# All four expert chunks of a batch in one full-array section, the expert bias beside the second scores, a turned mask in two buffers, and a new order of the first steps

## The chip, the cores and the metric

The kernel runs on one core of one Trainium2 chip. The metric is the device time of one execution in microseconds; of several runs the median is taken.

## The reference

A transformer block with adaptive layer norm over x of 16 batches, 256 tokens, 128 channels, all in fp32:

```
mod = silu(c) @ wmod -> sa, ca, ga, sb, cb, gb per batch (|ga|, |gb| at least 0.25)
h = layernorm(x) * (1 + ca) + sa
q, k, v = h @ Wqkv + bqkv                       # 16 heads of 8
K = exp(-r_sigma * (|k|^2 + |q|^2 - 2 k.q))      # no softmax: a Gaussian kernel
x = x + ga * ((K @ v) @ Wproj + bproj)
h = layernorm(x) * (1 + cb) + sb
gamma = softmax(h @ w_router.T + b_router)       # 8 experts
mask = the two largest of gamma, as 0 or 1
x = x + gb * sum over experts e of mask[e] * (h @ w_experts[e].T + b_experts[e])
```

## The kernel before

The five engines run programs of their own, written out by hand and tied by semaphores. Each program calls `step(k)` for k = -2 to 14, then `last()` for batch 15 and `tail()`. A step is a software pipeline over batches: step k computes the scores and exponentials of batch k, and beside them the projection of batch k-1, second norm and router of batch k-2, the experts of batch k-3, the bias and gate of batch k-4, and ahead of these the first norm and queries and keys of batch k+2 (GpSimd's `first_norm` of k+3). The order of the calls within `step` is the order in which each engine's queue works; nothing overtakes.

TensorE (PE). The four groups of scores of a batch, `qk_scores(k, g)`, each fill all four banks of `scores` with 8 matmuls on 32-row tiles (the trace's `32*128`). ScalarE empties them with two exponentials each, `exp(k, g, 0)` and `exp(k, g, 1)`, and TensorE waits for the first before it starts the next group and for the second before its third matmul. Attention times values (`pv`), queries and keys (`qk_rows`), `norms`, `values`, `router` and `project` work on 128-row, 32-column tiles (`128*32`); the experts and the turns (`turn_x`, `turn_x2`, `turn_mask`) use the array in full height and width. The expert bias is a matmul over 16 rows, `expert_bias`. An expert chunk is one call `experts(b, c)`: three matmuls of 512 columns (the high and low parts of the split weights and activations) into the bank that `f_bank` gives; four chunks make a batch. A PSUM bank is shared by several of these: chunk 1 lies in `att_ps`, where `pv` collects the heads, so chunk 1 stands between `heads_out` and `pv(k, 0)`.

VectorE (DVE) multiplies each chunk with the mask and accumulates it (`experts`, four instructions a chunk), copies the turned mask to SBUF (`mask_rows`), adds the norms' low parts (`norm_rows`), reads out queries and keys (`queries_keys`, `high_parts`), takes the logits and chooses, adds the residual, and normalises for the second norm. ScalarE (ACT) does the exponentials and small copies and norms between them (`norm_high`, `heads_out`, `keep_bias`, `first_norm`, `second_norm`). GpSimd (POOL) squares and splits queries and keys (`parts`), weighs the projection with the gate (`weigh(k)`, which waits for `project(k-1)`), computes the rstd (`rsqrt`), normalises for the first norm (`first_norm`) and applies the gate (`gate`). SyncE (SP) issues the DMAs: x, the stacked rows of queries and keys with their norms (`stack`), the gate rows and the stores.

Of the names that the prediction uses: k is the step, NB is 16, NC (chunks) 4, HE 4, STEPS 16 (VectorE's accumulations a batch, counted by `acc_step`), WIDE 13 (batches below it use the 512-column chunks).

## Time and profile before

| what | value |
|---|---|
| median of three runs | 225.05 us (223.19 to 225.72) |
| the profiled execution's own time | 224.27 us |
| its span in the trace | 222.4 us |
| PE busy | 207.9 us, 93% of the span |
| DVE busy | 173.2 us, 78% |
| ACT busy | 161.8 us, 73% |
| POOL busy | 155.5 us, 70% |
| mean granted clock of TensorE | 0.992 |

The span runs from the first to the last instruction of the profiled execution; the time of an execution has about 1.9 us around it. Busy times are of instructions as the profiler records them. TensorE's matmuls are pipelined, so a matmul's recorded duration overlaps the next one; distances between starts tell what a group costs. PE busy is therefore no measure of how near TensorE is to its peak.

### The profile page before, as it was taken

To read this page: it belongs to the slowest core of one execution; us is meant where nothing else is said; L and a number is where in the kernel's file an instruction comes from. 1 tells how busy PE (TensorE), PEld (TensorE's weight loads), DVE (VectorE), ACT (ScalarE), POOL (GpSimd) and SP (SyncE) were. 2 spreads that over 40 slices of the span, in tenths; PEclk is the share of its full clock that TensorE was granted. 3 is DMA by queue.
4 is the path that set the end of the run, shared out by engine and by line. 5 is a ranking of instruction groups with operands and counts; after the bars stand their busy time and mean duration, and the time that the engine had idled before them with its cause. 6 is when DMAs were issued, how large, how long until landed. Compare 5 with 4: busy or idle time off the path is not lost.

```text
span 222.4 us, 7993 instructions
## 1 busy us (share of the span) xinstructions
PE 207.9 (93%) x3084; PEld 138.7 (62%) x3084; DVE 173.2 (78%) x595; ACT 161.8 (73%) x233; POOL 155.5 (70%) x230
## 2 busy tenths in 40 slices
PE   7976869899999999999999999999999999989993
PEld 7553425466666676666666666666766767555792
DVE  4776703267989898898979898989898988897884
ACT  5228775888877878879796969697888788656362
POOL 4456955656596969696979889797979663745183
PEclk9999997999999999999999999999999999999999
DMA  4564233433332434342415151424223243000001
GB/s 147 154 208 153 97 124 95 142 115 109 99 116 68 144 98 144 93 149 73 163 52 192 30 182 41 155 84 137 102 84 131 71 143 99 3 24 27 3 24 47
DMA packets 22470, 22.91 MB, mean 103 GB/s; under 512 B 2330, under 2 KB 20258, under 8 KB 22434
## 3 DMA queue, kind: packets, MB, share of 16 engines
q1 hardware_dynamic: 21962, 21.79, 30.3%
q10 hardware_dynamic: 472, 0.62, 0.8%
q8 instruction: 25, 0.41, 0.8%
q14 instruction: 11, 0.09, 0.1%
HBM read 6.65 MB, written 2.12 MB: 39 GB/s over the span
## 4 chain that ended last, share of the span: by engine, by line
PE 82%; DVE 6%; POOL 4%; issue 3%; ACT 2%; DMA 1%; POOLq 0%; ACTq 0%
PE att_ps L1073 23%; PE scores L1053 11%; PE qkv_ps L1092 8%; PE ffn_ps L1250 4%; PE mid_ps L1148 3%; PE qkv_ps L1250 3%; PE ffn_ps L1252 3%; PE ffn_ps L1251 3%; PE mid_ps L1103 3%; PE qkv_ps L1116 3%; ACT probs L539 2%; PE scores L1005 2%; PE qkv_ps L1252 2%; PE qkv_ps L1251 2%; PE mid_ps L1162 1%
## 5 line engine op out<-in xcount | busy, mean ns | idle before, releaser
L539 ACT ACTIVATE probs<-scores 128x1024 f32<-128x1024 f32 x128 | 124.3, 1022 | 32.1 <-PE scores L1053 30.8
L1073 PE MATMUL att_ps<-probs,vpad 128*32 128x256 f32 x1024 | 65.5, 383 | 0.1
L1073 PEld LDWEIGHTS att_ps<-probs,vpad 128*32 128x32 f32 x1024 | 33.1, 111 | 16.8 <-issue 1.3
L1053 PE MATMUL scores<-st 32*128 32x256 f32 x512 | 35.3, 332 | 5.2 <-ACT probs L539 3.8
L435 POOL TENSOR_TENSOR sq<-qkf 128x512 f32<-128x512 f32 x15 | 15.6, 1040 | 31.9 <-DVE qkf L793 31.9
L1053 PEld LDWEIGHTS scores<-st 32*128 32x128 f32 x512 | 20.8, 183 | 21.1 <-issue 11.9
L768 DVE SCALAR_TENSOR_TENSOR acc<-ffn_ps,mask,acc 128x128 f32<-128x128 f32 x102 | 28.4, 340 | 0.0
L399 POOL TENSOR_SCALAR xn<-x_all,stats,rstd 128x128 f32<-128x128 f32 x30 | 24.3, 815 | 1.6
L394 POOL TENSOR_TENSOR rstd<-ve,expo 128x2 f32<-128x2 f32 x32 | 22.9, 715 | 2.5
L793 DVE TENSOR_TENSOR qkf<-qkv_ps,bqk_col 128x512 f32<-128x512 f32 x16 | 11.1, 692 | 12.0 <-PE qkv_ps L1092 10.8
L437 POOL TENSOR_TENSOR hl<-qkf,hl 128x512 fp32r<-128x512 f32 x15 | 19.2, 1282 | 0.0
L1092 PE MATMUL qkv_ps<-h,wqk_sb 128*32 128x256 f32 x256 | 18.8, 416 | 0.0
L765 DVE TENSOR_SCALAR acc<-qkv_ps,mask 128x128 f32<-128x128 f32 x26 | 7.9, 346 | 11.7 <-PE qkv_ps L1252 11.7
L748 DVE BATCH_NORM_STATS2 stats<-x_all 128x6 f32<-128x256 f32 x32 | 13.7, 427 | 0.6
L1250 PE MATMUL ffn_ps<-we_hi,h_hi 128*128 128x512 f32 (+1 forms) x30 | 14.0, 465 | 0.0
L427 POOL TENSOR_TENSOR x_all<-x_all,rb_all 128x256 f32<-128x256 f32 x16 | 12.8, 799 | 0.0
L392 POOL TENSOR_TENSOR ve<-stats,eps 128x2 f32<-128x2 f32 x32 | 6.3, 197 | 8.9 <-DVE stats L748 8.9
L425 POOL TENSOR_TENSOR wg<-wproj_sb,rb_all 128x128 f32<-128x128 f32 x16 | 7.8, 487 | 6.0 <-PE mid_ps L1148 5.9
L408 POOL TENSOR_TENSOR gated<-acc 128x256 f32<-128x256 f32 x13 | 9.7, 748 | 2.6 <-DVE acc L768 2.6
L1252 PE MATMUL ffn_ps<-we_lo,h_hi 128*128 128x512 f32 (+1 forms) x30 | 11.4, 379 | 0.0
L1251 PE MATMUL ffn_ps<-we_hi,h_lo 128*128 128x512 f32 (+1 forms) x30 | 11.4, 379 | 0.0
L411 POOL TENSOR_TENSOR gated<-gated,bias_sb 128x256 f32<-128x256 f32 x13 | 9.6, 736 | 2.5 <-ACT bias_sb L569 1.6
(188 smaller groups left out, 416.3 us busy)
## 6 DMA issues: line engine op xcount, KB each, us to landing
st<-hl SPq DMA_DIRECT2D x47, 256.0 KB
rb_all<-rb_rows SPq DMA_DIRECT2D x16, 192.0 KB, 3.4
out_dram<-x_all SPq DMA_DIRECT2D x16, 128.0 KB, 3.1
x_all<-in_L_attn_x_dram SPq DMA_DIRECT2D x13, 128.0 KB, 3.2
st<-norm_parts SPq DMA_DIRECT2D x60, 16.0 KB
we_sb<-in_L_ffn_w_experts_dram SPq DMA_DIRECT2D x1, 512.0 KB, 6.0
w_mod_sb<-in_L_wmod_dram SPq DMA_DIRECT2D x1, 256.0 KB, 5.3
st<-hl ACTq DMA_DIRECT2D x1, 256.0 KB
```

The source lines that it names most:

```text
L394: nc.gpsimd.tensor_tensor(rstd[:, n, :], ve[:, n, :], expo[:, :], ALU.pow).then_inc(rstd_ok, 1)
L399: i = nc.gpsimd.tensor_scalar(xn[:, par, t * C:(t + 1) * C], x_all[:, b, t * C:(t + 1) * C], stats[:, 0, par, 3 * t + 1:3 * t + 2], rstd[: ...
L435: nc.gpsimd.tensor_tensor(sq[:, :, :], qkf[:, :, :], qkf[:, :, :], ALU.mult).then_inc(sq_ok, 1)
L437: nc.gpsimd.tensor_tensor(hl[:, 1:4:2, :], qkf[:, :, :], hl_f[:, 0:4:2, :], ALU.subtract).then_inc(lo_ok, 1)
L539: nc.scalar.activation(probs[:, g, 2 * half:2 * half + 2, :], scores[:, 2 * half:2 * half + 2, :], ACT.Exp, scale=two_sigma).then_inc((exp ...
L768: v.scalar_tensor_tensor(a, y, m, a, ALU.mult, ALU.add).then_inc(acc_step, 1)
L1053: i = pe.matmul(scores[:, r, t * T:(t + 1) * T], st[rows, par, g, t * P:(t + 1) * P], st[rows, par, g, T:2 * T], start=True, stop=True)
L1073: i = pe.matmul(att_ps[r * ROWS:(r + 1) * ROWS, 0:T], heads[:, g * ROWS:(g + 1) * ROWS], probs[:, g, r, t * T:(t + 1) * T], start=(g == 0 ...
L1092: i = pe.matmul(qkv_ps[m, a * T:(a + 1) * T], wqk_sb[:, a, m], h1[:, b % 2, :], start=True, stop=True)
L1250: pe.matmul(dst, hi, we_hi[:, es], start=True, stop=False)
L1251: pe.matmul(dst, lo, we_hi[:, es], start=False, stop=False)
L1252: i = pe.matmul(dst, hi, we_lo[:, es], start=False, stop=True)
```

## The change

It moves work within the engines' lists and alters waits with it; no arithmetic changes.

- In a step from k = 3 on, TensorE works through all four chunks of batch k-3 in one section with the two turns of x, behind the second scores. Before, chunks 0 to 2 stood there and chunk 3 at the end of the step. The banks of the chunks are dealt anew (`f_bank`), and `pv(k, 0)` and `qk_rows` wait for one chunk more.
- `turn_mask` moves up behind the first scores, `expert_bias` behind the second scores; the turned mask `mask_t` gets two buffers. VectorE's `mask_rows` goes ahead of `norm_rows`, and its fourth chunk is taken right behind the third.
- From step 3 on, the projection goes from between the fourth scores and the product to the end of the list, `values` behind the second product, and the router stands ahead of them.
- ScalarE copies the bias between the two exponentials of group 1.
- In the first steps: the x of batches 4 and 5 are both loaded at k = 0; GpSimd normalises batches 2 and 3 before it weighs; the first norms of steps 1 and 2 go ahead of `parts`; `qk_rows(2)` stands behind the first scores of step 1 instead of ahead of them, with one product between the first and second and one behind the second scores; VectorE splits the expert weights and bias in step 1 instead of steps -1 and 0.

```diff
@@ PSUM banks and buffers
-        mask_t = sb("mask_t", [2 * NE, T], F32R)
+        mask_t = sb("mask_t", [2 * NE, 2, T], F32R)
...
-                return ((qkv_ps, att_ps, ffn_ps, ffn_ps) if b < NB - 4 else (qkv_ps, ffn_ps, qkv_ps, ffn_ps))[c][:, :]
+                return ((ffn_ps, qkv_ps, att_ps, ffn_ps) if b < NB - 4 else (qkv_ps, ffn_ps, qkv_ps, ffn_ps))[c][:, :]
@@ SyncE
-                if k >= 0 and has(k + 4):
-                    sp.dma_start(x_all[:, k + 4, :], xv[k + 4]).then_inc(ld_xb[k % 2], 16)
+                for b in (4, 5) if k == 0 else (k + 4,):
+                    if k >= 0 and k != 1 and has(b):
+                        sp.dma_start(x_all[:, b, :], xv[b]).then_inc(ld_xb[b % 2], 16)
@@ GpSimd (EARLY = 2)
                     parts(1)
                     first_norm(2)
-                    weigh(0)
                     first_norm(3)
                 if has(k - 4):
                     gate(k - 4)
+                if 0 < k <= EARLY:
+                    first_norm(k + 3)
                 if has(k + 2):
                     parts(k + 2)
-                if k > 0:
+                if has(k):
                     weigh(k)
...
-                if k > 0 and has(k + 3):
+                if k > EARLY and has(k + 3):
                     first_norm(k + 3)
@@ ScalarE
-                if k > 0:
+                if k > 1:
                     norm_high(k + 1)
-                if has(k - 1):
+                if k > 1:
                     heads_out(k - 1)
+                exp(k, 1, 0)
                 if has(k - 4):
                     keep_bias(k - 4)
-                exp(k, 1, 0)
                 exp(k, 1, 1)
-                if k == 0:
+                if k == 1:
+                    heads_out(k - 1)
+                if k <= 1:
                     norm_high(k + 1)
...
-                if k == 0:
-                    first_norm(k + 2)
...
                 exp(k, 3, 1)
+                if k == 0:
+                    first_norm(k + 2)
@@ VectorE (the expert bias' parts move from expert_weights to split_weights)
                 if k == 0:
                     first_stats(2)
+                if k == 1:
+                    first_stats(4)
+                if has(k - 3):
+                    mask_rows(k - 3)
                 if has(k + 1):
                     norm_rows(k + 1)
                 if has(k - 3):
-                    mask_rows(k - 3)
-                    experts(k - 3, 0)
-                    experts(k - 3, 1)
-                    experts(k - 3, 2)
+                    for c in range(NC):
+                        experts(k - 3, c)
                 if k == 0:
                     values(1)
                     first_stats(3)
+                if k == 1:
                     split_weights()
...
-                if k > 0 and has(k + 3):
+                if k == 1:
+                    first_stats(5)
+                if k > EARLY and has(k + 3):
                     first_stats(k + 3)
...
-                if has(k - 3):
-                    experts(k - 3, 3)
@@ TensorE, waits
                             if 3 <= b < NB - 1:
-                                pe.wait_ge(acc_step, STEPS * (b - 3) + 2 * HE)
+                                pe.wait_ge(acc_step, STEPS * (b - 3) + 3 * HE)
...
                 if b >= 5:
-                    pe.wait_ge(acc_step, STEPS * (b - 5) + HE)
+                    pe.wait_ge(acc_step, STEPS * (b - 5) + 2 * HE)
...
-                if b >= 3:
-                    pe.wait_ge(h2_ok, b - 2)
+                if b >= 4:
+                    pe.wait_ge(logit_ok, b - 2)
+                elif b == 3:
+                    pe.wait_ge(h2_ok, 1)
...
                 if b < NB - 4 and c == 0:
+                    pe.wait_ge(m_sb, b + 1)
+                elif b < NB - 4 and c == 1:
                     pe.wait_ge(norm_ok, b + 5)
-                elif b < NB - 4 and c == 1:
+                elif b < NB - 4 and c == 2:
                     pe.wait_ge(o_ok, b + 3)
-                elif b < NB - 4 and c == 2:
-                    pe.wait_ge(m_sb, b + 1)
                 elif b < NB - 4:
-                    pe.wait_ge(acc_step, steps(b, 3 * HE))
+                    pe.wait_ge(acc_step, steps(b, HE))
@@ TensorE, the order of a step
                 qk_scores(k, 0)
-                if has(k - 4):
-                    expert_bias(k - 4)
-                if k == 0:
+                if has(k - 3):
+                    turn_mask(k - 3)
+                if k <= 1:
                     qk_rows(k + 1)
                 if k > 1:
                     norms(k + 1)
                 if has(k - 1):
                     pv(k - 1, 2)
+                if k > 1:
                     pv(k - 1, 3)
+                qk_scores(k, 1)
+                if has(k - 4):
+                    expert_bias(k - 4)
                 if k == 1:
-                    norms(k + 1)
-                if has(k - 3):
-                    turn_mask(k - 3)
-                qk_scores(k, 1)
-                if k == 0:
+                    pv(k - 1, 3)
+                if k <= 1:
                     norms(k + 1)
                 if has(k - 3):
                     experts(k - 3, 0)
...
                 if has(k - 3):
                     experts(k - 3, 2)
+                    experts(k - 3, 3)
                 qk_scores(k, 2)
...
                 pv(k, 0)
-                values(k + 1)
+                if k < 3:
+                    values(k + 1)
                 if k == 0:
                     turn_x(k + 2)
                 if has(k - 2):
                     router(k - 2)
                 qk_scores(k, 3)
+                if k >= 3:
+                    pv(k, 1)
+                    values(k + 1)
                 if has(k - 1):
                     project(k - 1)
-                pv(k, 1)
+                if k < 3:
+                    pv(k, 1)
                 if k == NB - 2:
                     turn_mask(k - 2)
-                if k == 0:
-                    qk_rows(k + 2)
-                if has(k - 3):
-                    experts(k - 3, 3)
```

## Rows read from the trace of the kernel before

**Rows 1.** Busy by stage (steps 7, 14): us, PE, PEld, DVE, ACT, POOL, clock, DMA.

```profile
96.85:108.62 11.77, 11.76 (x189) 7.85 (x188) 10.29 (x37) 9.57 (x13) 9.66 (x16) 1.00 0.36 114
179.17:190.40 11.23, 11.11 (x175) 7.63 (x174) 9.17 (x36) 9.26 (x13) 5.37 (x11) 1.00 0.28 96
```

**Rows 2.** TensorE's timeline in step 7: start, length, instructions, idle time before in brackets.

```profile
96.85 0.51 PE L1053 MATMUL scores<-st 32*128 32x256 f32 x8
...
97.45 0.43 PE L1116 MATMUL qkv_ps<-sq,nw 128*32 128x128 f32 x8
...
99.76 0.51 PE L1053 MATMUL scores<-st 32*128 32x256 f32 x8
100.19 0.51 PE L1250 MATMUL qkv_ps<-we_hi,h_hi 128*128 128x512 f32 x1
...
100.99 0.40 PE L1250 MATMUL att_ps<-we_hi,h_hi 128*128 128x512 f32 x1
...
101.70 0.38 PE L1162 MATMUL mid_ps<-ident,x2n 128*128 128x128 f32 x2
...
102.93 0.51 PE L1053 MATMUL scores<-st 32*128 32x256 f32 x8
...
105.12 0.62 PE L1103 MATMUL mid_ps<-wqkv_sb,h 128*32 128x128 f32 x16
105.56 0.29 PE L1172 MATMUL mid_ps<-wr_t,h 128*32 128x8 f32 x16
105.77 0.51 PE L1053 MATMUL scores<-st 32*128 32x256 f32 x8
106.29 0.64 PE L1148 MATMUL mid_ps<-wg,o_sb 128*32 128x128 f32 x16
106.72 1.07 PE L1073 MATMUL att_ps<-probs,vpad 128*32 128x256 f32 x16
107.72 0.50 PE L1250 MATMUL ffn_ps<-we_hi,h_hi 128*128 128x512 f32 x1
...
108.62 0.51 PE L1053 MATMUL scores<-st 32*128 32x256 f32 x8
```

**Rows 3.** ScalarE's timeline: pairs of exponentials in steps 0, 1, 2 and 7.

```profile
18.55 1.94 ACT L539 ACTIVATE probs<-scores 128x1024 f32<-128x1024 f32 x2 [0.49 <-PE scores L1053]
...
26.84 1.94 ACT L539 ACTIVATE probs<-scores 128x1024 f32<-128x1024 f32 x2 [0.49 <-PE scores L1053]
...
39.90 1.94 ACT L539 ACTIVATE probs<-scores 128x1024 f32<-128x1024 f32 x2 [0.50 <-PE scores L1053]
...
103.47 1.94 ACT L539 ACTIVATE probs<-scores 128x1024 f32<-128x1024 f32 x2
```

**Rows 4.** TensorE's timeline in steps 0 and 1.

```profile
18.11 0.50 PE L1053 MATMUL scores<-st 32*128 32x256 f32 x6 [0.53 <-ACT probs L539]
...
20.54 0.50 PE L1053 MATMUL scores<-st 32*128 32x256 f32 x6 [0.53 <-ACT probs L539]
...
23.48 0.44 PE L1135 MATMUL mid_ps<-ident,xn 128*128 128x128 f32 x2 [1.00 <-POOL xn L399]
...
33.07 1.94 PE L1092 MATMUL qkv_ps<-h,wqk_sb 128*32 128x256 f32 x16
```

**Rows 5.** Busy time by stage, as rows 1, around the slower clock.

```profile
32.80:36.30 3.50, 3.50 (x38) 1.65 (x38) 1.04 (x2) 2.10 (x3) 0.46 (x1) 0.51 0.38 122
```

**Rows 6.** VectorE's timeline: values in step 0; residual, chunk 3 and mask copy in step 7.

```profile
22.54 0.42 DVE L817 TENSOR_TENSOR vpad<-mid_ps,bq_all 128x256 f32<-128x256 f32 x1 [1.44 <-PE mid_ps L1103]
...
95.74 0.41 DVE L825 TENSOR_TENSOR x_all<-mid_ps,x_all 128x256 f32<-128x256 f32 x1
...
97.21 1.10 DVE L768 SCALAR_TENSOR_TENSOR acc<-ffn_ps,mask,acc 128x128 f32<-128x128 f32 x4
...
99.86 0.41 DVE L841 CAST mask_t<-ffn_ps 16x256 fp32r<-16x256 f32 x1
```

**Rows 7.** The page's slices: TensorE's granted clock in tenths, 40 slices of the span.

```profile
PEclk9999997999999999999999999999999999999999
```

16 lines of the change are left out of this document (8 added, 8 removed).

## The prediction

> **What bounds the kernel now.** I read the profile by stages, since the kernel is a start, a pipeline of 16 equal batches and an end. The busy times of one step of the pipeline come first: in the step from 96.85 to 108.62 us TensorE is busy 11.76 of 11.77 us, VectorE 10.29, ScalarE 9.57, GpSimd 9.66 [rows 1]. TensorE sets that step. The timeline of TensorE in the same step shows it working through its list with no idle bracket at all [rows 2]. I divide the step at its four groups of scores, because each of them hands ScalarE two exponentials (together 1.94 us, [rows 3]) and the next group of scores may overwrite its banks only after they are done. The four distances are 2.91 us (96.85 to 99.76), 3.17 (to 102.93), 2.84 (to 105.77) and 2.85 (to 108.62) [rows 2]. The question for the change is not only how much TensorE work it removes, but in which of these four distances.
>
> How short can a distance get? In the first step ScalarE sets the pace: the six matmuls that need the second exponential start at 18.11 and again at 20.54 after 0.53 us idle, which is a cycle of 2.43 us: 0.44 from these matmuls to the first exponential (18.55), 1.94 of exponentials, 0.05 back [rows 3, 4]. When the eight matmuls of a group run without a stop, the first exponential starts 0.54 after them (102.93 to 103.47), so the distance behind an undisturbed group is at least 0.54 + 1.94 + 0.05 = 2.53 us [rows 2, 3]. All four distances now are above that.
>
> The early steps are another matter. The exponentials of batch 1 begin at 26.84 and those of batch 2 at 39.90, so this step takes 13.06 us [rows 3]. In it the granted clock is 0.51 from 32.8 to 36.3, about the lower of its two levels (1.2 against 2.4 GHz), and the 16 matmuls of the queries and keys, started at 33.07, take 1.94 us [rows 4, 5]. In step 0 the turn of x, at 23.48, waits 1.00 us for GpSimd's normalised rows [rows 4].
>
> **The change part by part: the steady step** (k from 4 to 13, ten steps). TensorE's new list, priced by distances of starts in rows 2.
>
> First distance: scores, turned mask, norms, two attention products. The bias product leaves. Before, scores and bias took 0.60 (96.85 to 97.45); now the scores stand alone at 0.43 (as 99.76 to 100.19). Norms, products and mask keep 2.31 (97.45 to 99.76). Sum 2.74, 0.17 less.
>
> Second distance: scores and bias 0.60, first chunk 0.80 (100.19 to 100.99), then everything up to 102.93 as before (1.94), then the fourth chunk. A chunk inside a full-array section is 0.71 (100.99 to 101.70). Sum 0.60 + 0.80 + 1.94 + 0.70 = 4.04, which is 0.87 more.
>
> Third distance: the values (0.44, 105.12 to 105.56) go. TensorE alone would need 2.40. ScalarE's bound is 2.53, and that is what counts: 0.31 less.
>
> Fourth distance: before, scores 0.52 (with some 0.08 of waiting for the logits), projection 0.43, product 1.00 and the lone chunk 0.90 (107.72 to 108.62). Now scores 0.43, product 0.86, values 0.44, projection about 0.55 with its way out, in all 2.29. The lone chunk cost 0.90 against 0.70 in company. ScalarE's cycle after scores that had to wait is 2.43: 0.42 less.
>
> Sum over TensorE's work alone: 2.74 + 4.04 + 2.40 + 2.29 = 11.47, which is 0.30 under 11.77. Sum with ScalarE: 2.74 + 4.04 + 2.53 + 2.43 = 11.74, only 0.03 under. So the saved changes of tile shape are real, but the fourth chunk is taken from a distance that then falls under ScalarE's bound and is put into one that has ScalarE idle anyway. Ten steps give 0.3 us. The prices of the mask behind scores and of the bias ahead of a chunk are not shown by rows in this order; I take their neighbours' and allow 0.06 a step each way, 0.6 us in all.
>
> A rule that speaks to these changes. The same three matmuls take 0.90 where they stand alone and 0.71 inside a section, and the product ahead of the lone chunk needs 1.00 where the work itself is some 0.86 (102.93 to 105.12 is scores, 0.44, and two groups of 16 such matmuls, 1.75: queries and keys 0.89, product 0.86), so entering and leaving the full array costs about 0.1 each time [rows 2]. The Trainium skill, TensorEngine Tiling (Array Packing), section Tiling Modes, says that changing the tiling mode, and not just the tile, drains TensorE; by that rule alone the ten steps would give 3 us. The trace agrees that there is a price; what it is worth is another question, and the rule's own result is the second rival below.
>
> Waits inside the steady step. VectorE takes the chunks in turn, four accumulations in 1.10 us each, of which the next hides 0.07 [rows 6]. Its first begins about 1.0 us after the start of chunk 0, so chunk 0 is read out before chunk 3 wants its bank (0.5 us to spare), chunk 1 before the queries and keys of the next batch (0.7), chunk 2 before the next product (0.6). VectorE has no work more than before. The projection moves to the end of the list, just ahead of the next scores, and behind it hang the residual, the second norm's statistics, GpSimd's weighting and rstd, the normalised rows and only then the turned mask's copy, which chunk 0 now waits for. Before, residual to mask copy was 4.12 us (95.74 to 99.86), with the fourth chunk (1.03) and the norm rows (0.26) in between, which both go [rows 6]: 2.8 us remain, 0.4 more for the copy. The residual starts some 0.16 after the next scores do, so the copy is there at 3.3, and chunk 0 is due at 2.74 + 0.60 = 3.34. It just fits. I price this at nothing, with the third rival in mind. ScalarE's moves (bias copy between the exponentials of group 1) lie in its idle time of the long second distance.
>
> **Steps 3 and 14, and the end.** Step 3 has no bias yet: nothing. Step 14 (11.23 us, rows 1) has no queries and keys and its bias product sits in the third distance. There the fourth chunk lengthens the second distance by 0.87 as well; first distance 2.74, second 3.82, third 2.53 (ScalarE again), fourth 2.51 with the last turned mask: 11.60, so 0.37 more. The end is not edited, but its first turn of x2 needs rows that hang on the late projection of step 14; between nothing and one chunk (0.9, rows 2) I take 0.3 more.
>
> **The early steps.** Step 0: the statistics of batch 2 no longer stand behind VectorE's work on the expert bias, and GpSimd normalises it before the weighting. GpSimd is free 0.5 us sooner; then the turn of x waits for VectorE to have read the values (its add ends at 22.96, [rows 6]) instead of for GpSimd: from 23.48 to 23.02, 0.46 less. The second x load moves one step up on SP's queue, ahead of the stacking of batch 1; an issue is about 0.45 us and the low parts behind it come later anyway, so nothing. ScalarE's h of batch 2, moved behind the last exponential, fits into the 0.44 between scores and exponential.
>
> Step 1, by the four distances. First: scores, queries and keys, one product is 2.19 + 0.11 for leaving (102.93 to 105.12 is the same work), under ScalarE's 2.43. Second: product 1.00, norms 0.24, turn of x 0.36 and scores 0.43, again under 2.43; the squares that the norms need come from GpSimd 0.3 earlier than wanted, where the old order kept TensorE idle. Third: TensorE waits until ScalarE has copied heads and norms and made h of batch 3 (0.93 after the scores), then queries and keys 0.89, product 0.86 and values with their way out 0.55: 3.24. Fourth: 2.53. Sum 10.63 against 13.06, so 2.43 less. About 1.5 of it is the half-speed stretch: at full speed those 1.94 us would be 1.07 and the product behind would lose as much. I take it that it goes, because the 3 us ahead of the drop hold a product and most of a group of queries and keys more in the new order. VectorE's 3.4 us of splitting the expert weights move into step 1, ahead of its work on batch 3's queries and keys. By this count that work starts between 34 and 34.9, and the norms that need it come at 37.0; the split hides, with 0.2 us to spare.
>
> Step 2 keeps its four distances.
>
> **Sum.** 224.27 (the profiled execution; its span is 222.4 and 1.9 lies around it) - 0.46 - 2.43 - 0.3 + 0.37 + 0.3 = 221.75. The median of the three runs is 225.05, 0.78 above the profiled execution, and the three spread over 2.5 us, so I place the forecast a little above the sum: 222.0.
>
> **The rivals.**
> First, the half-speed stretch stays or comes at another place. For it: the new order of step 0 still leaves TensorE idle up to 0.9 us before the second exponential. Against: the stretches with that much idle before 26 us kept full clock, and the page shows only this drop [rows 7]. Price 1.5 us: 223.5. Chance 0.16. The Trainium skill, TensorE: Matmul & The Clock Gate, Part 1, says that the throttled state is the default and activity releases it; the trace shows the drop after the stretch with the least TensorE work.
> Second, ScalarE doesn't bind and the drains saved count in full: 0.27 more in each of ten steps, 219.0. For it: ScalarE is idle 0.9 us before most exponentials. Against: rows 4 show the cycle of 2.43 when nothing else holds. Chance 0.11.
> Third, the other side: the late projection. If the way from projection over rstd to the mask copy is longer than my 3.3 us, chunk 0 waits, and the second distance, which has no slack, grows by all of it. It decides from 0.05 us on. At 0.3 us a step it costs 3 us and eats the gain: 224.8; at 0.6, with the drop of the clock kept, 229. For it: the fit is within 0.1 us, and the same instructions of VectorE and GpSimd vary with what the other does. Chance 0.17, of which 0.08 ends above 227.3.
> Fourth, the early reorder brings only the 0.46 of step 0, because another wait (the stacked rows' DMA or the split weights) holds step 1: 224.2. Chance 0.12.
> The forecast itself, 221.0 to 223.2, has 0.44.
>
> **How the numbers follow.** The range must take in 8 of 10: from 219.2 (most of the second rival) to 225.2 (the first, the fourth and the middle of the third). Differences under about 1% can't be told from no change here; 1% faster is 222.8. Faster: 0.9 of the forecast's 0.44, the second rival and a fifth of the first, 0.54. Slower than 227.3: 0.08 to 0.09. The rest, 0.37, is no change.
>
> **What would show it.** In the new trace the step of 11.77 should be 11.7 to 11.8; scores at distances of about 2.7, 4.0, 2.5 and 2.4; TensorE with idle brackets of 0.1 to 0.2 us on ScalarE's exponentials before the fourth and the first scores of a step, where it has none now. The exponentials of batches 1 and 2 should be 10.6 apart, without a stretch at half clock. Step 14 should be near 11.6. If chunk 0 shows an idle bracket that names the mask copy, the third rival is at work; a step of 11.5 would be the second. The forecast is wrong as a whole if the early gain doesn't come, since nearly all of it lies there.

## The result, and the profile after

| | before | after |
|---|---|---|
| median of the runs taken together | 224.12 us (4 runs, 223.09 to 225.72) | 226.56 us (4 runs, 225.15 to 227.78) |
| the profiled execution | 224.27 us, span 222.4 | 225.99 us, span 224.1 |
| its mean granted clock | 0.992 | 0.985 |

The ratio is 1.0107, 95% interval 1.0054 to 1.016: the change makes the kernel about 1% slower. The forecast was 222.0 us, 1.4% faster, and the range ended at 225.2. Here and below, ratios and their intervals leave out executions more than 1.5% above the fastest of their kernel (two of six of the early order alone, three of six of the same with the norm rows first, one each of four others: the mask copy first, that early order filled, the turn of the mask moved, and the kernel before beside the first experiments), while medians take in all.

The span is best compared by steps. A step is taken here from the third matmul of its first scores (the one that waits for ScalarE's second exponential) to that of the next. The last 0.05 us, closing semaphores, are left out.

| stretch | before | after | forecast for after |
|---|---|---|---|
| start to the first scores | 15.58 | 14.64 | as before |
| step 0 | 10.82 | 12.22 | 10.36 |
| step 1 | 13.06 | 10.69 | 10.63 |
| step 2 | 10.45 | 11.80 | as before |
| step 3 | 11.60 | 11.56 | as before |
| steps 4 to 13, each | 11.77 | 11.81 | 11.74 |
| step 14 | 11.23 | 12.23 | 11.60 |
| from the first scores of batch 15 to the end | 31.90 | 32.79 | 32.2 |

The differences are -0.94, +1.40, -2.37, +1.35, -0.04, +0.40 (ten steps), +1.00 and +0.89, in all 1.69 us; the spans differ by 1.7. The code of the first 14 us is the same in both, so the 0.94 of the start belongs to no edit. Nearly all of it lies in one group, the first queries and keys, which start at 7.23 us in both and take 1.90 us before and 1.07 after (TensorE's timeline).

```profile
7.23 1.90 PE L1092 MATMUL qkv_ps<-h,wqk_sb 128*32 128x256 f32 x16
```

```profile
7.23 1.07 PE L1099 MATMUL qkv_ps<-h,wqk_sb 128*32 128x256 f32 x16
```

Over all kernels below, the start varied from 14.2 to 15.6 us and this group from 1.07 to 1.94: up to 14.7 us where it took 1.07 us, from 15.4 where it took 1.87 or more. What makes it long is open: the same 16 matmuls take 1.94 us at half clock in step 1 [rows 4, 5], but here the granted clock is recorded as 1.00.

The steady step first: busy times of the new steps 7 and 14, as [rows 1]. These two stretches begin at the first matmul of a group that stops in its middle, so they are longer than the steps by their third matmuls (step 14 by 0.12 us).

```profile
96.20:108.02 11.82, 11.79 (x194) 8.12 (x190) 10.44 (x36) 9.60 (x14) 9.77 (x14) 1.00 0.33 114
178.90:191.25 12.35, 11.34 (x180) 7.92 (x176) 8.66 (x34) 9.47 (x14) 5.17 (x8) 1.00 0.28 97
```

And TensorE's timeline in step 7, as [rows 2].

```profile
96.20 0.63 PE L1060 MATMUL scores<-st 32*128 32x256 f32 x8
...
99.06 0.51 PE L1060 MATMUL scores<-st 32*128 32x256 f32 x8
99.40 0.33 PE L1217 MATMUL mid_ps<-be_parts,mask_t 16*128 16x128 f32 x2
99.76 0.47 PE L1259 MATMUL ffn_ps<-we_hi,h_hi 128*128 128x512 f32 x1
...
103.17 0.51 PE L1060 MATMUL scores<-st 32*128 32x256 f32 x8
...
105.57 0.64 PE L1060 MATMUL scores<-st 32*128 32x256 f32 x8
...
108.02 0.39 PE L1060 MATMUL scores<-st 32*128 32x256 f32 x2
```

By the third matmul of each group the distances are 2.74, 4.11, 2.53 and 2.43 us (by first matmuls they look like 2.86, 4.11, 2.40, 2.45, since a group that is stopped in its middle starts early). The third and the fourth are ScalarE's cycle to the hundredth: its pairs of exponentials begin at 103.72, 106.15 and 108.58, 2.43 apart, idle 0.49 between them. The records show the stop not as a bracket but as the first row of a group that is 0.63 us long instead of 0.51.

From the bias product (99.40) to chunk 0 (99.76) there are 0.36 us; in a run below, where nothing holds the chunk, there are 0.26. VectorE's timeline of these moments shows what it waits for.

```profile
98.12 0.42 DVE L855 TENSOR_TENSOR h_lo<-h,h_hi 128x256 fp32r<-128x256 f32 x1
98.69 0.60 DVE L837 TENSOR_SCALAR x2n<-x_all,stats,rstd 128x128 f32<-128x128 f32 x2
99.21 0.41 DVE L843 CAST mask_t<-ffn_ps 16x256 fp32r<-16x256 f32 x1
```

The mask copy ends at 99.62 and stands behind the normalising, which can't start before GpSimd's rstd ends at 98.66. In step 14 the same wait is in the open, and behind it a product waits for VectorE's accumulations (TensorE's timeline; before, the step had neither bracket). The second wait costs nothing: the third distance of the step, where it lies, is 2.53 us before and after.

```profile
182.99 0.47 PE L1259 MATMUL ffn_ps<-we_hi,h_hi 128*128 128x512 f32 x1 [0.56 <-DVE mask_t L843]
...
187.31 1.07 PE L1080 MATMUL att_ps<-probs,vpad 128*32 128x256 f32 x16 [0.45 <-DVE acc L770]
```

The early steps: ScalarE's pairs of exponentials in steps 0, 1 and 2, as [rows 3]. The wait of 2.69 us lies in step 0.

```profile
17.61 1.94 ACT L542 ACTIVATE probs<-scores 128x1024 f32<-128x1024 f32 x2 [0.50 <-PE scores L1060]
...
24.86 1.94 ACT L542 ACTIVATE probs<-scores 128x1024 f32<-128x1024 f32 x2 [2.69 <-PE scores L1060]
27.30 1.94 ACT L542 ACTIVATE probs<-scores 128x1024 f32<-128x1024 f32 x2
...
37.99 1.94 ACT L542 ACTIVATE probs<-scores 128x1024 f32<-128x1024 f32 x2 [0.49 <-PE scores L1060]
```

From 27.30 to 37.99 step 1 takes 10.69 us, as forecast, and without a stretch at half clock. But the page's slices, and the busy times of the stretch in question, show that half clock now lies in step 0, and for twice as long.

```profile
PEclk9995899999999999999999999999999999999999
```

```profile
17.40:24.20 6.80, 5.52 (x56) 2.73 (x52) 2.15 (x6) 4.04 (x5) 4.49 (x7) 0.50 0.57 193
```

Step 2 has a new wait. TensorE's timeline first, then VectorE's.

```profile
45.66 0.51 PE L1060 MATMUL scores<-st 32*128 32x256 f32 x8
47.90 0.64 PE L1157 MATMUL mid_ps<-wg,o_sb 128*32 128x128 f32 x16 [1.73 <-DVE logit L862]
```

```profile
41.29 0.60 DVE L837 TENSOR_SCALAR x2n<-x_all,stats,rstd 128x128 f32<-128x128 f32 x2 [2.47 <-POOL rstd L396]
41.80 0.34 DVE L812 SCALAR_TENSOR_TENSOR norm_parts<-norm_hi,lo_col,qkv_ps 128x128 fp32r<-128x128 f32 x1
44.40 0.69 DVE L795 TENSOR_TENSOR qkf<-qkv_ps,bqk_col 128x512 f32<-128x512 f32 x1 [2.25 <-PE qkv_ps L1099]
46.98 0.69 DVE L801 TENSOR_TENSOR hl<-qkv_ps,bqk_col 128x512 fp32r<-128x512 f32 x1 [1.90 <-DMA st<-norm_parts]
47.59 0.17 DVE L862 TENSOR_TENSOR logit<-mid_ps,br_all 128x16 f32<-128x16 f32 x1
```

Read from below: the projection waits for the logits, whose bank it writes; the logits stand on VectorE behind the high parts of batch 4; these wait for the DMAs that stack the norm rows of batch 3, four issues that SP's queue took from 42.17 to 44.93; and these rows (41.80) stand behind the normalising of batch 0, which sat 2.47 us for rstd.

The end: TensorE's first turn of x2 there, and what it waits for on VectorE.

```profile
195.25 0.44 PE L1171 MATMUL mid_ps<-ident,x2n 128*128 128x128 f32 x2 [0.74 <-DVE x2n L837]
```

```profile
191.16 0.42 DVE L827 TENSOR_TENSOR x_all<-mid_ps,x_all 128x256 f32<-128x256 f32 x1 [1.51 <-PE mid_ps L1157]
...
193.64 1.55 DVE L837 TENSOR_SCALAR x2n<-x_all,stats,rstd 128x128 f32<-128x128 f32 x2 [0.27 <-POOL rstd L396]
```

### The profile page after: what moved, and what is told of

Same layout as the page of the kernel before. It is cut to its first block, busy times and chain, and to the rows that moved or that the text cites. A ratio compares the mean times of both kernels' runs of the same rounds, so it can differ in the third digit from the quotient of the medians.

```text
span 224.1 us, 7993 instructions
## 1 busy us (share of the span) xinstructions
PE 207.6 (93%) x3084; PEld 142.1 (63%) x3084; DVE 173.8 (78%) x595; ACT 162.2 (72%) x233; POOL 156.9 (70%) x230
## 4 chain that ended last, share of the span: by engine, by line
PE 75%; POOL 8%; DVE 7%; issue 3%; DMA 3%; ACT 2%; SPq 1%; POOLq 0%; DVEq 0%
PE att_ps L1080 21%; PE scores L1060 11%; PE qkv_ps L1099 6%; PE ffn_ps L1259 4%; PE mid_ps L1112 3%; PE ffn_ps L1261 3%; PE ffn_ps L1260 3%; PE mid_ps L1157 3%; DMA st<-norm_parts 3%; ACT probs L542 2%; DVE acc L770 2%; PE qkv_ps L1125 2%; PE scores L1012 2%; POOL rstd L396 2%; PE mid_ps L1171 2%
## 5 line engine op out<-in xcount | busy, mean ns | idle before, releaser
L1080 PEld LDWEIGHTS att_ps<-probs,vpad 128*32 128x32 f32 x1024 | 31.3, 110 | 19.1 <-issue 1.4
L1060 PE MATMUL scores<-st 32*128 32x256 f32 x512 | 38.2, 335 | 3.1 <-ACT probs L542 1.8
L1060 PEld LDWEIGHTS scores<-st 32*128 32x128 f32 x512 | 23.6, 184 | 21.1 <-issue 15.2
L437 POOL TENSOR_TENSOR sq<-qkf 128x512 f32<-128x512 f32 x15 | 15.6, 1042 | 25.8 <-DVE qkf L795 25.8
L396 POOL TENSOR_TENSOR rstd<-ve,expo 128x2 f32<-128x2 f32 x32 | 25.1, 785 | 2.5
L770 DVE SCALAR_TENSOR_TENSOR acc<-ffn_ps,mask,acc 128x128 f32<-128x128 f32 x78 | 22.4, 342 | 0.0
L767 DVE TENSOR_SCALAR acc<-ffn_ps,mask 128x128 f32<-128x128 f32 x26 | 7.9, 346 | 10.8 <-PE ffn_ps L1261 10.8
L837 DVE TENSOR_SCALAR x2n<-x_all,stats,rstd 128x128 f32<-128x128 f32 x32 | 11.4, 399 | 5.0 <-POOL rstd L396 3.6
L770 DVE SCALAR_TENSOR_TENSOR acc<-att_ps,mask,acc 128x128 f32<-128x128 f32 x48 | 13.4, 342 | 0.0
L875 DVE TENSOR_SCALAR mask<-taken 128x32 fp32r<-128x32 f32 x16 | 12.7, 794 | 0.6
L801 DVE TENSOR_TENSOR hl<-qkv_ps,bqk_col 128x512 fp32r<-128x512 f32 x15 | 10.2, 683 | 3.3 <-DMA st<-norm_parts 3.3
```

The costliest lines, as they stand in the source:

```text
L396: nc.gpsimd.tensor_tensor(rstd[:, n, :], ve[:, n, :], expo[:, :], ALU.pow).then_inc(rstd_ok, 1)
L437: nc.gpsimd.tensor_tensor(sq[:, :, :], qkf[:, :, :], qkf[:, :, :], ALU.mult).then_inc(sq_ok, 1)
L770: v.scalar_tensor_tensor(a, y, m, a, ALU.mult, ALU.add).then_inc(acc_step, 1)
L875: v.tensor_scalar(mask[:, b % 2, :, :, :], taken[:, :, :].unsqueeze(2).broadcast_to([P, NT, 2, NE]), CHOSEN, None, ALU.is_ge).then_inc(mas ...
L1060: i = pe.matmul(scores[:, r, t * T:(t + 1) * T], st[rows, par, g, t * P:(t + 1) * P], st[rows, par, g, T:2 * T], start=True, stop=True)
L1080: i = pe.matmul(att_ps[r * ROWS:(r + 1) * ROWS, 0:T], heads[:, g * ROWS:(g + 1) * ROWS], probs[:, g, r, t * T:(t + 1) * T], start=(g == 0 ...
```

## The experiments

My theory after the result: the loss is four separate things, each with a cause of its own: the norm rows of batch 3 late in step 2, the mask copy behind the normalising (a little in each step, 0.6 us in step 14), the late projection of step 14, which the end waits for, and half clock in step 0, which I put down to TensorE's idle time there. The rival theory: the new order of the steady steps as such is dearer for TensorE than I count (the saved changes of tile shape aren't worth what I took), and what shows as waits would only move elsewhere if mended.

**First, the two halves of the change, and the first two repairs** (timed together; before had a median of 224.97 us beside them).

The early order alone is the kernel before with the edits that mention `EARLY`, k <= 1, k == 0 and k == 1 in the diff; the steady order alone is the changed kernel with these undone.

> The kernel before with only the first steps reordered (loads of x, GpSimd, ScalarE, VectorE and TensorE in steps 0 and 1); the steady step is that of before, 11.77 us. My theory now: of the loss, step 2 is an early one (scores of batch 2 to scores of batch 3 took 11.80 us after against 10.45 before, because the chain from the norms of batch 2 over the stacked rows' DMA to the logits of batch 0 did not come earlier), and step 1 keeps its gain (10.69 against 13.06). Steps 0 to 3 together end within 1 us of before at the same number of slow clock windows: 223 to 224.5 in all. Rival, that the early order is where the whole loss lies: 226 or more. Rival, my prediction's: about 221.5.

> The changed kernel with the order of the first steps put back to that of before. The steady step was 11.81 us after against 11.77 before, step 14 12.23 against 11.23, and the end 32.85 against 32.0: sum +2.3, so this should be about 2.3 us slower than before (226.4), with the same step of 11.81 and distances of scores 2.74, 4.11, 2.53, 2.43. Rival, that the late reorder costs nothing and the loss is the clock's in the first steps: equal to before within 0.5 us.

The mask copy first:

```diff
-                if has(k - 3):
-                    mask_rows(k - 3)
                 if has(k + 1):
                     norm_rows(k + 1)
...
                 if has(k - 2):
                     split_h2(k - 2)
+                    mask_rows(k - 2)
                 if has(k - 1):
                     normalise(k - 1)
```

> The changed kernel with VectorE's copy of the turned mask ahead of the second norm's normalised rows instead of behind them. My theory: chunk 0 waits for this copy, 0.08 us in each steady step and 0.56 us in step 14, because it stands behind GpSimd's rstd. Expected: the second distance 4.03 instead of 4.11 and the step 11.73; step 14 at 11.7 instead of 12.23; 1.3 us less than the changed kernel. Rival, that chunk 0 is late because the bias product ahead of it on the array needs that long to leave: nothing changes in the steady step.

The norm rows first:

```diff
-                if has(k + 1):
+                if has(k + 1) and k != 2:
                     norm_rows(k + 1)
...
+                if k == 1:
+                    norm_rows(3)
                 if has(k - 1):
                     normalise(k - 1)
```

> The changed kernel with VectorE's norm rows of batch 3 ahead of the normalised rows of batch 0 (the first of which waited for nothing but the latter's rstd). My theory: in step 2 the norm rows came at 41.8 us behind that wait, their DMAs landed at 46.9, and behind this landing VectorE's high parts of batch 4 and the logits of batch 0 held the projection 1.73 us. With the norm rows at 40.2 the projection waits 0.2 to 0.5 and the scores of batch 3 come 1.1 us earlier. Rival, that GpSimd's chain holds the step whatever VectorE's order: no change of that distance (3.67 us).

Measured (the steps and the end are those of each kernel's one profiled execution):

| kernel | median us | ratio to before, interval | step 0 | 1 | 2 | 4 to 13 | 14 | end |
|---|---|---|---|---|---|---|---|---|
| early order alone | 223.7 | 0.994 (0.9883 to 0.9996) | 10.41 | 10.69 | 12.32 | 11.76 | 11.23 | 31.92 |
| steady order alone | 226.71 | 1.0098 (1.005 to 1.0146) | 10.82 | 13.04 | 10.44 | 11.81 | 12.23 | 33.90 |
| mask copy first | 223.67 | 0.9981 (0.9922 to 1.0041) | 10.41 | 10.69 | 12.09 | 11.74 | 11.62 | 32.76 |
| norm rows first | 225.0 | 1.0038 (0.9982 to 1.0094) | 11.80 | 10.69 | 10.63 | 11.81 | 12.23 | 32.75 |

The early order gains 0.6%, the steady order loses 1%. Where no half clock falls on it, the early order brings 10.41 and 10.69 us for steps 0 and 1, 2.8 us less than before (whose step 1 holds a half-clock stretch), and gives back 1.6 in step 2 (12.09 in the third row; the 12.32 of the first has 3.41 us of half clock in it, behind which the wait of the projection is hidden). With the norm rows first, step 2 is 10.63 and the wait of the projection is gone, where I had expected 0.2 to 0.5 us of it to stay. With the mask copy first, chunk 0 follows the bias product after 0.26 us (TensorE's timeline, step 7), the ten steps are 0.07 us shorter each and step 14 is 0.61 shorter: 11.62 where I had worked out 11.60.

```profile
98.07 0.51 PE L1059 MATMUL scores<-st 32*128 32x256 f32 x8
98.41 0.33 PE L1216 MATMUL mid_ps<-be_parts,mask_t 16*128 16x128 f32 x2
98.67 0.50 PE L1258 MATMUL ffn_ps<-we_hi,h_hi 128*128 128x512 f32 x1
...
102.11 0.51 PE L1059 MATMUL scores<-st 32*128 32x256 f32 x8
```

The median fell by more than these 1.3 us, from 226.56 to 223.67. The clock goes with that: the profiled execution had no half clock in its early steps, and four of the six had a mean clock of 0.992 or more, against one of four of the changed kernel. The end of 33.90 in the steady order alone holds a stretch of 3.41 us at half clock, from 202.6 on.

**Second, what the steady step is bound by.** In both kernels the exponentials of groups 2 and 3 run over half their columns. The other half is left out, so these kernels compute something else, and each ran once; only the steps are compared.

```diff
-                nc.scalar.activation(probs[:, g, 2 * half:2 * half + 2, :], scores[:, 2 * half:2 * half + 2, :], ACT.Exp,
+                w = NT * T // 2 if g >= 2 and k > 0 else NT * T
+                nc.scalar.activation(probs[:, g, 2 * half:2 * half + 2, 0:w], scores[:, 2 * half:2 * half + 2, 0:w], ACT.Exp,
```

> The changed kernel, in which from batch 1 on the exponentials of the third and fourth group of scores run over 512 of their 1024 columns (the other half of these exponentials is left out). If ScalarE's cycle of 2.43 to 2.53 us is what keeps the third and fourth distance long, both fall to TensorE's own work there: 2.41 and 2.29 us, and the steady step goes from 11.81 to 11.5 to 11.6 us. If instead the saved changes of tile shape never were worth anything in these two distances, or something else holds them (logits, heads, a DMA), the step stays at 11.8 us. The early steps and the end gain as well, so the time as a whole (some 4 to 6 us less) decides nothing; the step does.

> The kernel before with the same half of the exponentials left out. If its steady step is set by TensorE in all four distances, the step stays at 11.75 to 11.78 us although ScalarE has 1.9 us a step less to do; then the two kernels with half exponentials differ by about 0.2 to 0.27 us a step in favour of the changed order, ten steps by 2 to 2.7 us. If ScalarE takes part in the limit of the old order as well, its step falls too, by 0.1 us or more, and the difference is smaller.

The old order keeps 11.76 us: TensorE alone sets it (the first two distances, whose exponentials were left whole, are 2.90 and 3.17, above ScalarE's 2.53). The new order falls from 11.81 to 11.69: that is neither the 11.5 to 11.6 of the expectation nor the 11.8 of its rival. TensorE's timeline shows why:

```profile
96.82 0.51 PE L1061 MATMUL scores<-st 32*128 32x256 f32 x8
...
99.56 0.51 PE L1061 MATMUL scores<-st 32*128 32x256 f32 x8
99.90 0.33 PE L1218 MATMUL mid_ps<-be_parts,mask_t 16*128 16x128 f32 x2
100.39 0.47 PE L1260 MATMUL ffn_ps<-we_hi,h_hi 128*128 128x512 f32 x1 [0.16 <-DVE mask_t L844]
...
103.80 0.51 PE L1061 MATMUL scores<-st 32*128 32x256 f32 x8
...
106.20 0.51 PE L1061 MATMUL scores<-st 32*128 32x256 f32 x8
...
108.52 0.51 PE L1061 MATMUL scores<-st 32*128 32x256 f32 x8
```

The third and fourth distance fell to 2.40 and 2.31, as expected of TensorE's own work. But the first scores no longer stop in their middle, so what follows comes 0.12 us earlier after their start, while the mask copy ends 3.42 us after that start as before. Chunk 0 waits 0.13 us longer: half of the gain went into the mask copy. So the same cut was made once more with the mask copy first.

> The changed kernel with the mask copy ahead of the normalising and, as before, the exponentials of the third and fourth group over half of their columns from batch 1 on (half of these exponentials is left out). In the run with half exponentials alone the third and fourth distance fell to 2.40 and 2.32 us, but the second grew from 4.11 to 4.24, with chunk 0 waiting for the mask copy. If these are the only two things between the step and TensorE's own work, the step is 2.74 + 4.04 + 2.40 + 2.32 = 11.50 us. If something else comes late as soon as the mask copy is there, it stays at 11.6 us or more.

11.61 us, again not all. The distances are 2.74, 4.16, 2.41 and 2.31. Three are TensorE's own; in the second the turn of x stands 0.29 us behind the turn of x2 instead of 0.22, and its neighbour another 0.05, and GpSimd's timeline has the rows for which it waits end at 99.74, just ahead of it.

```profile
99.50 0.38 PE L1171 MATMUL mid_ps<-ident,x2n 128*128 128x128 f32 x2
99.79 0.44 PE L1144 MATMUL mid_ps<-ident,xn 128*128 128x128 f32 x2
```

```profile
98.16 1.58 POOL L401 TENSOR_SCALAR xn<-x_all,stats,rstd 128x128 f32<-128x128 f32 x2
```

So behind ScalarE and the mask copy stands a third cover (something that takes up a gain of TensorE's), GpSimd's way from the projection over the residual's weighting and the two rstd to the normalised rows. It is read from the trace, here and once more below; no run removes it. Without all three, TensorE's list would take 2.74 + 4.04 + 2.41 + 2.31 = 11.50 us, 0.26 less than the old order (this sum is of distances from two runs, not itself run).

**Third, the end.**

```diff
                 qk_scores(k, 3)
+                if k == NB - 2:
+                    project(k - 1)
                 if k >= 3:
                     pv(k, 1)
+                if 3 <= k < NB - 2:
                     values(k + 1)
-                if has(k - 1):
+                if has(k - 1) and k < NB - 2:
                     project(k - 1)
```

(and `values(15)` behind the first product of step 14, where it was before the change.)

> The changed kernel with one step put back: in step 14 the projection of batch 13 stands ahead of the product again, and the values of batch 15 where they stood. If the 0.85 us that the end has grown hang on the late projection of step 14 (residual, statistics, rstd and normalised rows of batch 13 follow it, and the end's first turn of x2 waits for them), the end falls from 32.8 to between 31.9 and 32.2 us, and the wait of that turn for the normalised rows goes. The rival: the end has grown since GpSimd's gate now runs beside VectorE's normalising there, or since the chunks are dealt to other banks; then it stays within 0.2 us of 32.8. Step 14 itself: 12.2 to 12.3 us either way, as its chunk waits for the mask copy.

The end took 31.89 us, as before the change, and the turn of x2 has no bracket left. Step 14 grew to 12.36, a little above the 12.2 to 12.3 expected. VectorE's normalising was 1.56 us long here too, beside GpSimd's gate, and it cost nothing, for it now started a projection's lead earlier: the rival is out. The time of this one run, 228.04 us, is of half clock for 13.7 us in the first 53; its stages afterwards are as the table has them.

**Fourth, the repairs together, and TensorE's idle time filled.** The fill is 3 warm-up matmuls of 128 columns ahead of the first scores, and in a free bank 1, 1 and 2 in step 0 and 4 in step 2.

```diff
+            def fill(n):
+                pe.wait_ge(wet0_sb, 1)
+                warm_up(n, bank=ffn_ps)
...
+                if k == 0:
+                    fill(1)
                 qk_scores(k, 1)
...
                     norms(k + 1)
+                if k == 0:
+                    fill(1)
+                if k == 2:
+                    fill(4)
...
                 if k == 0:
+                    fill(2)
                     turn_x(k + 2)
```

> The changed kernel with both repairs of VectorE's list: the mask copy ahead of the normalising, the norm rows of batch 3 ahead of the first normalising. If the two losses are what they seem, they add: steps of 11.73 us, step 14 at 11.6, step 2 at 10.6 instead of 11.8, so 1.3 us less than the first repair alone where the clock does the same: 222.2 us at a mean clock of 0.992, a median between 221.5 and 223.0 with one half-clock stretch in some runs. The rival: with the wait in step 2 gone a half-clock stretch comes in its place (as in the run with the norm rows first, 225.0), and the median is 223.5 or more.

> The kernel before with the new order of the first steps and the norm rows of batch 3 ahead of the first normalising; the steady steps are the old ones. Against the early order alone (223.7 us, its step 2 12.32 us with a half-clock stretch in it) the wait for the logits goes; step 2 should be 10.6 us without a half-clock stretch and 11.9 with one. Time 221.5 to 223, so 0.99 of before. If the wait was hidden behind the half-clock stretch, nothing is gained on the early order alone.

> As both copies first, and TensorE's idle time in the start and in steps 0 and 2 is filled with warm-up matmuls into a free bank (3 before the first scores, 1 before the second and 1 before the third scores, 2 before the turn of x in step 0, 4 before the turn of x2 in step 2). If the half-clock stretches of the first 50 us come from TensorE's idle time, they go: mean clock of the runs 0.99 to 1.0, and the time is that of both copies first at its best clock, 221.5 to 222.3 us, with less spread. If the stretches don't depend on this idle time, clock and spread stay and the time is the same or up to 0.5 us longer, for the added matmuls.

> As both filled, and the projection of step 14 ahead of the product again. If the end's growth is its doing, 0.5 to 0.9 us less than both filled: 220.7 to 221.7 us; else the same as both filled.

> The changed kernel with nothing but the warm-up matmuls in TensorE's idle time of the start and of steps 0 and 2. If the half-clock stretches of the first 50 us come from that idle time, the mean clock goes from 0.985 to 0.992 or more and the time from 226.6 to 224.5 to 225.3 us; the waits in step 2, for the mask copies and at the end stay. If they don't, it stays at 226 to 227 us.

> The kernel before with the new order of the first steps, the norm rows of batch 3 first, and TensorE's idle time in the start and in steps 0 and 2 filled with the same warm-up matmuls. Its steady steps, its step 14 and its end are those of before: 10 x 11.76 + 11.22 + 31.9. Against both filled with the early projection of step 14 (221.7 us; 10 x 11.74 + 11.75 + 31.9) that is 0.3 us less: 221.4 us at a mean clock of 1.0. So if the steady change has nothing to give on this chip as it stands, this kernel is as fast or faster, 221.0 to 221.8; if it has, this one is 222 or more. If the half-clock stretches don't come from the idle time, the runs spread from 221 to 225 as with the early order and the norm rows alone.

| kernel | median us (lowest to highest, runs) | ratio to before, interval | mean clocks |
|---|---|---|---|
| both copies first | 223.68 (222.13 to 225.16, 12) | 0.9974 (0.9934 to 1.0014) | 0.977 to 1.0, two of 12 at 1.0 |
| early order, norm rows first | 224.03 (220.91 to 225.27, 6) | 0.9897 (0.9822 to 0.9972) | 0.974 to 1.0 |
| both copies first, filled | 222.68 (221.97 to 224.81, 12) | 0.9951 (0.991 to 0.9992) | 0.981 to 1.0, three at 1.0 |
| the same, early projection in step 14 | 221.7 (221.44 to 222.04, 6) | 0.988 (0.9829 to 0.9931) | 1.0 in five of 6 |
| changed kernel, filled | 225.11 (223.97 to 226.97, 12) | 1.0032 (0.9995 to 1.007) | 0.989 to 1.0 |
| early order, norm rows first, filled | 221.27 (220.64 to 224.94, 6) | 0.9867 (0.9815 to 0.9919) | 1.0 in four of 6 |

Not all expectations came. Both copies first was to be at 221.5 to 223.0 us; at 223.68, with a half-clock stretch in step 2 of its profile, it met its rival's case. The early order with the norm rows first was expected at 221.5 to 223 and both filled at 221.5 to 222.3; their medians lie above. The other three came as expected. The ratio of the second row rests on three executions.

The fill: the changed kernel's median is 225.11 us with it and was 226.56, in four runs on another occasion, without; the intervals of the two ratios overlap, and so they do in the other two pairs of this table with and without the fill. Full clock for the whole span came in no run of four without the fill and three of 12 with it (changed kernel), two of 12 and three of 12 (both copies first), one of six and four of six (early order, norm rows first). So the fill seems to help, and that isn't shown for any one kernel. It doesn't keep half clock away: the profiled executions of the changed kernel filled and of both filled still have one stretch of 3.41 us in step 0 (11.90 and 11.96 us). Step 2 of the changed kernel filled took 12.18 us, not 11.80; why is open. Both copies first, by the stages of its profile: 10.41, 10.69, 12.33 (half clock in it), 11.74 each, 11.62, 32.78; step 2 without half clock is 10.62 in the filled one. With the early projection step 14 is 11.75 and the end 31.90. By stages, then, the repairs add up as worked out; the medians have the clock's draws in them as well.

The last row is the answer on the steady change: with the same repairs of the first steps, the old steady order (11.76 a step, 11.23 in step 14, 31.91 at the end) is 221.27 us and the new one, with its own two repairs, 221.7. The ratios' intervals overlap, so neither is shown to be faster than the other; no gain of the steady change is shown.

**Fifth, work moved under the bound.** On the fully repaired kernel the turn of the mask goes one step earlier, behind the projection.

```diff
-                if has(k - 3):
-                    turn_mask(k - 3)
...
-                if k == NB - 2:
+                if has(k - 2):
                     turn_mask(k - 2)
```

> Both filled with the early projection of step 14 (221.7 us), and the turn of the mask one step earlier, behind the projection: its 0.22 us go from the first distance (2.74 us, above ScalarE's bound) into the fourth (2.43 us, where ScalarE sets the pace and TensorE's own work is 2.3). If the bounds of the distances are as the runs so far show, the step goes from 11.74 to 2.53 + 4.04 + 2.53 + 2.51 = 11.61 to 11.65 us, and the time to 220.4 to 221.0 us. If the turn there waits for the choice of the experts, or ScalarE's bound isn't what holds the fourth distance, the step stays at 11.74 us or grows.

221.92 us (220.55 to 225.2, 12 runs), ratio 0.9889 (0.9851 to 0.9928); steps of 11.74 and 11.83 us by turns. The expected 0.1 us a step didn't come. The distances of step 7 are 2.53, 4.24, 2.53 and 2.53, three of them as expected; the second grew by 0.2: the turn of x, due 0.22 us after the turn of x2, came after 0.38, when GpSimd's normalised rows were there.

```profile
98.60 0.38 PE L1173 MATMUL mid_ps<-ident,x2n 128*128 128x128 f32 x2
98.98 0.44 PE L1146 MATMUL mid_ps<-ident,xn 128*128 128x128 f32 x2
```

```profile
97.34 1.58 POOL L402 TENSOR_SCALAR xn<-x_all,stats,rstd 128x128 f32<-128x128 f32 x2
```

ScalarE's bounds held: the fourth distance took the turn for 0.1 us, the first gave 0.21. The third cover, found with the half exponentials, is what the gain ran into by the trace.

## Why the prediction was wrong, point by point

- **"Step 2 keeps its four distances"** failed: +1.35 us, the largest single error. I followed what step 1 would gain and not what its gain would ask of the next step. TensorE came to step 2 1.9 us sooner; GpSimd, with the first norm of batch 4 now ahead of `parts(3)`, gave rstd 3.7 us after the step's third matmul (41.25 against 37.55) where before it was 0.8 after it. VectorE's norm rows stood behind that, then SP's four issues, the high parts, the logits, the projection. With the norm rows ahead, step 2 was 10.63: the wait is shown to be the cause. That the order of `first_norm(4)` and `parts(3)` is what made rstd late is read from the trace, and wasn't tried alone.
- **"I price this at nothing" (the fit of the mask copy)** failed: the third rival, in a small form, 0.07 us a step, and 0.6 of step 14, which I had left out of that rival. The terms were right and the addition was not: 0.16 to the residual, 2.83 (4.12 - 1.03 - 0.26) and 0.41 for the copy make 3.40, not 3.3, so by its own terms the copy came after the 3.34 at which chunk 0 was due. Measured in step 7: 0.14, 2.87 and 0.41, in all 3.42. The copy ahead of the normalising gave back both, and then the step (11.74) and step 14 (11.62) were the forecast's 11.74 and 11.60.
- **"between nothing and one chunk (0.9, rows 2) I take 0.3 more" (the end)** was mis-sized: 0.89. It was the upper bound that held, and the cause was the one named, the late projection of step 14.
- **Half clock: "I take it that it goes"** held for step 1 and failed for the kernel. In the profiled execution 6.83 us of half clock lie in step 0, the first rival's case. They cost 1.8 us (12.22 against 10.41 in profiles of the same order without half clock) instead of 1.5. The price of one stretch was right: 3.41 us of half clock made step 0 11.80 to 11.96 instead of 10.41, and step 2 12.33 instead of 10.62, which is 1.4 to 1.7 us.
- **What the half clock belongs to.** How much of it there is differs between executions of one kernel. Of 58 runs of the kernel before, timed beside the experiments, 19 had a mean clock of 0.992 and a median of 223.17 us, 33 had 0.977 and 225.07: a mean clock lower by 0.015 went with 1.9 us more. One stretch of 3.41 us makes 0.992 of this span, as in the profile. But none of the 58 had a higher clock than 0.992, and the three profiles with the old order of the first steps (before, steady order alone, half exponentials) all have a stretch in step 1, beginning between 31.9 and 32.9 us. With the new order of the first steps and no fill, three of 41 runs had full clock (half exponentials not counted). So one stretch seems to belong to the old order, and the new one can lose it; the mistake was to take its loss as sure in every execution and to price nothing for others. That TensorE's idle time brings it isn't shown. The Trainium skill, TensorE: Matmul & The Clock Gate, Part 1, has activity release the throttled state; by that rule the fill should help, and the runs lean that way without showing it.
- **The steady step** was right in its mechanism and, with the mask copy mended, in its size. Distances of 2.74, 4.04, 2.53 and 2.43 were measured for 2.74, 4.04, 2.53 and 2.43. The gain of 0.26 us in TensorE's own work, worked out above as 11.50 against 11.76, is hidden by ScalarE in two distances. The second rival is out as a result, though its price, 0.27 a step, was right. The Trainium skill, TensorEngine Tiling (Array Packing), section Tiling Modes, says that a change of the mode drains TensorE; the traces agree in that the order with one full-array section fewer a step needs these 0.26 us less of TensorE.
- **Steps 0 and 1** were right where the clock was full: 10.41 for 10.36, 10.69 for 10.63, and in step 1 in each distance (2.43, 2.43, 3.30 and 2.53 for 2.43, 2.43, 3.24 and 2.53). But of the 2.4 us of step 1, some 1.5 were the clock's; no profile has the old step 1 at full clock, so this is an estimate from the prices of a stretch above.
- **The sum.** Forecast -2.5 us against the profiled execution, measured +1.7 in it: +1.35 (step 2), +1.86 (step 0), +0.7 (steady steps), +0.63 (step 14), +0.6 (end), less 0.94 of a shorter start, make 4.2.
- **The chances.** The clock (first rival), the mask copy (third) and the end's upper bound were taken as alternatives, one at a time, and a wait for the stacked rows' DMA only for step 1 (fourth). They lie in different steps and nothing ties them; three came true together, and the DMA's wait one step later. Independent risks of one sign belong in the range as a sum.

## What to carry to other kernels

When an edit makes an engine arrive earlier somewhere, the next step must be priced with the other engines where they were, not moved along: ask of each wait in it what is queued ahead of the releaser. An order change pays only in distances that the changed engine alone sets; divide the step at the points of exchange and give each distance its own bounds, for a gain met here three covers in turn (ScalarE, a copy on VectorE, GpSimd). Half clock in a profile is partly a draw: price a stretch apart from the steps, look in several executions at how often it comes, and put the draw into the range, for the new order as well as for the old.

## What the runs showed that I had not expected

- The same VectorE instruction, two normalisings of 128x128, took 0.60 us in steady steps and 1.12 us at the end of the kernel before; at the end of the changed kernels it took 1.55 and 1.56. At these ends GpSimd's gate ran beside it each time (in the kernel before from 0.15 us after its start), so the gate alone doesn't explain 1.55 against 1.12. GpSimd's own 128x256 products took 0.73 in the changed kernel's gate. The last instruction of VectorE's choice of experts (128x32) took 1.01 us in a steady step of the kernel with the mask copy first, 0.61 in step 2 of the changed kernel, and 0.18 in its step 14, where GpSimd was idle.
- With warm-up matmuls in its idle time TensorE kept full clock for the whole span in 22 of 48 runs of five kernels, without them in three of 41. The fully repaired kernel had it in five of six, and a spread of 0.6 us (221.44 to 222.04), against 2.1 to 6.2 for the others that ran six times or more; with the turn of the mask moved, the same kernel had it in seven of 12 and spread over 4.7 us, so the 0.6 is also luck of six runs.
- A group of matmuls that stops in its middle for a semaphore shows no idle bracket in a long step: its row is 0.63 us instead of 0.51. In the old order no row of scores in step 7 is longer than 0.51, and that told that ScalarE didn't hold it.
